# Graph layer, aggregation stage: two sets of scatter matrices, and the second visit of each node tile written ahead of the loop

## The reference

```
xn = layernorm(x)
x  = x + gnn(xn, edges) + mix(xn)
x  = x + moe_ffn(layernorm(x))

gnn(xn): h = xn @ W.T;  e = leaky_relu(h@a_src [src] + h@a_dst [dst])
         alpha = softmax of e over the edges (and one self loop) of each dst
         out[n] = sum over edges with dst = n of alpha * h[src]
         return xn + elu(out + bias)
mix(xn): linear attention, 8 heads, relu(q), relu(k); out / max(q . sum k, 100); projection
moe_ffn: 8 experts, two per row, relu MLP, layernorm, gates
```

## Time and profile before

| | us |
|---|---|
| median of 3 runs | 2688.14 (2682.47 to 2689.73) |
| the profiled execution | 2689.04 |
| its span | 2687.3 |
| PE busy in the span | 2450.9 (91%) |
| DVE busy in the span | 1624.5 (60%) |
| POOL busy in the span | 1283.5 (48%) |

### The profile page before, as it was taken

One profiled execution on the slowest core, in us unless ns is written; L12 is line 12 of the kernel. 1 busy time (PEld: TensorE's weight loads), 2 busy tenths in 40 slices (PEclk: granted clock), 3 DMA queues, 4 the chain that ended last, 5 costly groups with the idle time before them and its releaser, 6 DMA issues. The chain is left out here.

```text
span 2687.3 us, 53608 instructions
## 1 busy us (share of the span) xinstructions
PE 2450.9 (91%) x12032; PEld 1387.6 (52%) x12033; DVE 1624.5 (60%) x4117; ACT 902.2 (34%) x1583; POOL 1283.5 (48%) x1272
## 2 busy tenths in 40 slices
PE   3999899999999889999999999999999639999995
PEld 2555577766666423333444444444444326777773
DVE  2655466664222244466666666666667575889886
ACT  0333344442111100011122222323333426677774
POOL 1444520000000477777776666555545154777774
PEclk9999899999999899999999999999999759999998
DMA  4333733331001477777777776666666355777775
GB/s 177 127 128 123 97 110 101 103 103 33 24 24 32 129 207 213 211 219 227 243 241 224 217 212 207 206 207 197 197 193 205 137 192 102 130 131 132 132 129 82
DMA packets 178069, 409.96 MB, mean 153 GB/s; under 512 B 46749, under 2 KB 46781, under 8 KB 176930
## 3 DMA queue, kind: packets, MB, share of 16 engines
q0 software_dynamic: 90512, 280.63, 40.0%
q1 hardware_dynamic: 59074, 76.65, 10.3%
q10 hardware_dynamic: 28368, 51.41, 5.6%
HBM read 339.65 MB, written 68.82 MB: 152 GB/s over the span
## 5 line engine op out<-in xcount | busy, mean ns | idle before, releaser
L1056 POOL DMA_INDIRECT rows<-h_rows,src_col x784 | 783.8, 1000 | 481.4 <-PE acc_ps L1159 228.8
L1159 PE MATMUL acc_ps<-rows,W 128*128 x1776 | 838.8, 611 | 59.1 <-DVE W L1257 33.2
L1159 PEld LDWEIGHTS acc_ps<-rows,W 128*128 128x128 f32 x1776 | 310.9, 190 | 527.0 <-issue 526.4
L1257 DVE TENSOR_SCALAR W<-window,dst_col,w_col 128x128 f32<-128x128 f32 x888 | 300.3, 372 | 314.5 <-PE acc_ps L1159 263.5
L1635 POOL DMA_INDIRECT out<-y,idx_add x105 | 168.5, 1605 | 112.4 <-issue 47.1
L649 POOL DMA_DIRECT2D alpha_d<-score x1 | 0.6, 573 | 461.8 <-DVE score L967 461.8
L1085 ACT ACTIVATE a_sd<-a_mv,cst 128x1 f32<-128x1 f32 x49 | 14.4, 295 | 606.6 <-DVE a_mv L1323 606.6
L1679 PE MATMUL o_ps<-w,hidT 128*128 x420 | 202.7, 605 | 7.4 <-DVE z L1739 3.2
L1669 PE MATMUL hid_ps<-xsT,w_now 128*128 128x128 f32 x1680 | 206.7, 277 | 0.2 <-issue 0.2
L1669 PEld LDWEIGHTS hid_ps<-xsT,w_now 128*128 128x128 f32 x1680 | 197.8, 194 | 1.0 <-issue 1.0
L773 PEld LDWEIGHTS q_ps<-hxnT,wqkv 128*128 128x128 f32 x1568 | 182.4, 193 | 11.9 <-issue 11.9
(11 more groups left out here) (303 smaller groups left out, 3470.2 us busy)
## 6 DMA issues: line engine op xcount, KB each, us to landing
lo_row<-src_lo SPq DMA_DIRECT2D x98, 256.0 KB, 3.3
xb<-in_x SPq DMA_DIRECT2D x49, 256.0 KB, 2.7
h_rows<-kb SPq DMA_DIRECT2D x49, 256.0 KB
fold_w<-in_x SPq DMA_DIRECT2D x49, 256.0 KB
rows<-h_rows,src_col POOLq DMA_INDIRECT x784, 3.8
a_own<-h_rows ACTq DMA_DIRECT2D x49, 256.0 KB, 3.8
a_xr<-in_x ACTq DMA_DIRECT2D x49, 256.0 KB, 5.2
out<-a_x ACTq DMA_DIRECT2D x49, 256.0 KB, 4.7
```

What stands on the lines that cost most here:

```text
L1056: nc.gpsimd.indirect_dma_start(G[:, n % ROWS, :], None, h_rows, bass.IndirectOffsetOnAxis(ap=src_col[:, n:n + 1], axis=0)).then_inc(row_in ...
L1159: nc.tensor.matmul(acc_ps[s][:], W[:, j, :], G[:, ds(row, 1), :].rearrange("p o d -> p (o d)"), start=(opens and j == 0), stop=(j == VT - ...
L1257: nc.vector.tensor_scalar(W[:, j, :], window[:], dst_col[:, ds(at_tile + j, 1)], w_col[:, ds(at_tile + j, 1)], ALU.is_equal, ALU.mult).the ...
```

## The change

W becomes two sets, `W_open` for the opening visit and `W_rest` for all others. The second visit of each node tile leaves the loop: on PE it stands behind `spread(t+1)` and ahead of `turn` and `denominators`, on DVE behind the opening visit and ahead of `scaled_q`. The loops begin at start + 2. DVE's wait on `row_used` for the two visits in front now asks for the visit two before (`after` = 0), and in the loop for the visit one before (`after` = 1); the semaphore begins 2 * VT ahead in place of VT. The setup stage gives each node tile at least 3 visits, clamps the first edge tile to ET - 3 * VT, and adds 1 + 2 * VT in `used_by`.

```diff
-rout[:, 4:6], rout[:, 0:2], float(ET - 2 * VT), None, ALU.min
+rout[:, 4:6], rout[:, 0:2], float(ET - 3 * VT), None, ALU.min
-rout[:, 3:4], rout[:, 2:3], 2.0, None, ALU.max
+rout[:, 3:4], rout[:, 2:3], 3.0, None, ALU.max
-used_by[:], use_ps[0:1, 0:FREED], float(1 + VT), ...
+used_by[:], use_ps[0:1, 0:FREED], float(1 + 2 * VT), ...
-            W = sb(ag, "W", [P, VT, P])
+            W_open, W_rest = (sb(ag, n, [P, VT, P]) for n in ("W_open", "W_rest"))
 (PE)
                     def visit(v, at_tile, s, opens):
+                        W = W_open if opens else W_rest
...
                                 spread(t + 1, 1 - s)
+                            visit(start + 1, first + VT, s, False)
                             if not isinstance(t, int) or t < NT - 3:
                                 turn(t + 3)
...
-                            with pe.Fori(start + 1, stop) as v:
+                            with pe.Fori(start + 2, stop) as v:
 (DVE)
-                    dve.sem_inc(row_used, VT)
+                    dve.sem_inc(row_used, 2 * VT)
-                    def visit(v, at_tile, opens):
+                    def visit(v, at_tile, W, after):
-                            dve.wait_ge(row_used, VT * v + j + 1)
+                            dve.wait_ge(row_used, VT * (v + after) + j + 1)
-                        if opens:
+                        if W is W_open:
-                            visit(start, first, True)
+                            visit(start, first, W_open, 0)
+                            visit(start + 1, first + VT, W_rest, 0)
                             scaled_q(t, s)
...
-                            with dve.Fori(start + 1, stop) as v:
-                                visit(v, tile_at(v), False)
+                            with dve.Fori(start + 2, stop) as v:
+                                visit(v, tile_at(v), W_rest, 1)
```

More of the change, by code:

```diff
@@ L358, in _ @@
                         step.settle()
-                        step.done(nc.vector.tensor_scalar(rout[:, 4:6], rout[:, 0:2], float(ET - 2 * VT), None, ALU.min))
+                        step.done(nc.vector.tensor_scalar(rout[:, 4:6], rout[:, 0:2], float(ET - 3 * VT), None, ALU.min))
                         step.settle()
@@ L370, in _ @@
                         step.settle()
-                        step.done(nc.vector.tensor_scalar(rout[:, 3:4], rout[:, 2:3], 2.0, None, ALU.max))
+                        step.done(nc.vector.tensor_scalar(rout[:, 3:4], rout[:, 2:3], 3.0, None, ALU.max))
                         assert step.n == 14
@@ L385, in _ @@
                         dve.wait_ge(tri, 2)
-                        nc.vector.scalar_tensor_tensor(used_by[:], use_ps[0:1, 0:FREED], float(1 + VT), C["freed"][0:1, :], ALU.add, ALU.add).then_inc(ints, 1)
+                        nc.vector.scalar_tensor_tensor(used_by[:], use_ps[0:1, 0:FREED], float(1 + 2 * VT), C["freed"][0:1, :], ALU.add, ALU.add).then_inc(ints, 1)
             with ExitStack() as nm:
@@ L542, in load @@
                     for k in range(n):
-                        first = nc.s_assert_within(eng.snap(found[2 * k] & ((1 << AT_BITS) - 1)), 0, ET - 2 * VT,
-                                                   skip_runtime_bounds_check_because="the setup stage takes the minimum with ET - 2 * VT")
+                        first = nc.s_assert_within(eng.snap(found[2 * k] & ((1 << AT_BITS) - 1)), 0, ET - 3 * VT,
+                                                   skip_runtime_bounds_check_because="the setup stage takes the minimum with ET - 3 * VT")
                         stop = eng.snap((visits_to + (found[2 * k] >> AT_BITS)) & 0xFFFF)
```

## The result

The changed kernel took 2706.28 us (median of 6 runs, 2701.97 to 2709.62) where the kernel before took 2688.93 (2682.47 to 2691.84): a ratio of 1.007, 95% interval 1.0058 to 1.0083. Forecast were 2729 us, +40.8; measured are +17.4. The direction, the place and the waiting engine were right; the size was 2.3 times too large. The stated range, 2700 to 2745, does hold the measured time, but not by the main case, whose own range began at 2712: it had been widened for rival B, which didn't happen.

The account below looks back on a forecast made before the run. PE was taken to bound the aggregation from tile 7 on, the gathers before. Spread's waits, 34.9 us in tiles 7 to 39 plus 5.9 in 40 to 48, gave +40.8 on 2689.04, forecast 2729 us allowing for the median; range 2700 to 2745.

Parts of the forecast that it names:

- main case: Aggregation: PE's spread waits for DVE's late qd, +40.8 us, 2729 us, own range 2712 to 2739; chance 0.69.
- rival B: Even openings: their waits absorb the 0.99 us spread wait of each odd tile, +24 us, 2712 us; chance 0.08.
- the tail: Node tiles 40 to 48: later spread, partly given back behind tiles of 3 visits, costs 5.9 us.
- Rival A: Even openings: the wait is for a free W buffer, so W_open removes it, about 2657 us; chance 0.10.
- D: Spread: qd comes in time after all, or the waits hide elsewhere; no change, 2688 +- 8 us; chance 0.07.
- C: PE's clock: added waits halve it in even tiles 8 to 38, 27 us on top, 2756 us; chance 0.06.
- the second visit ahead of scaled_q: DVE: qd ends later, so PE's spread waits 1.13 us in even, 0.99 in odd tiles; 34.9 us over tiles 7 to 39.
- gap in front of W_rest: DVE, between the copy to w_sum and the second visit's first W: taken as 0.53 us, bounds 0.15 and 0.71.

Follow-up runs that it names:

- e2: The changed kernel with the second visit back in the loop on PE and DVE, only the two sets of W kept: 2694.25 us, ratio 1.0009.
- f1: The changed kernel with scaled_q back ahead of the second visit and DVE's x2 block one iteration later: 2658.07 us, ratio 0.9877.
- f2: The kernel before with two sets of W, second visit in the loop, and DVE's x2 block one iteration later: 2674.68 us, ratio 0.9966.
- f3: The kernel before (one set W, second visit in the loop) with DVE's x2 block one iteration later: 2678.68 us, ratio 0.9957.
- e3: The changed kernel with one set W for all visits, the second visit still ahead of scaled_q: 2794.47 us, ratio 1.0387.
- g1: f1 with one set W in place of two: 2799.62 us, ratio 1.0433.
- e4: The changed kernel with PE's spread(t+1) moved behind the second visit, ahead of turn; DVE unchanged: 2686.43 us, ratio 0.9984.
- g2: The changed kernel, order untouched, with DVE's x2 block one iteration later: 2651.4 us, ratio 0.9876.

## Why the prediction was wrong in its size
Of the 23.4 us between forecast and result, 16.7 lie in tiles 7 to 39 and 3.7 in the tail; the rest is of the size by which executions differ in tiles 0 to 6.

**Right.** PE is late at the even openings by DVE's own queue, and W_open alone gives nothing (e2, f1, f2 against f3). No visit was added. `spread` waits for `qd` in some 40 node tiles (39). Three of them are tiles 3, 4 and 6 (0.32, 0.89 and 0.76 us), where the gathers still set the pace; they don't lengthen that stretch, as I had said, and e3's seven waits there barely do. POOL's waits stand nearly as in the earlier trace rows. The wait isn't given back at the even openings (rival B): those waits stand at 1.2 to 1.9 us in tiles 8 to 40, with 0.77 at tile 18 the one exception; from 8 to 40 they sum to 24.2 us against 24.9 before. Rival A is excluded by e2, D by the interval of the result. C did not happen in the changed kernel: one visit at half clock (tile 28, behind a wait of 1.91), as one before (tile 18):
```profile
1769.16 4.54 PE L1160 MATMUL acc_ps<-rows,W_open 128*128 x6 [1.91 <-DVE W_open L1259]
```
```profile
1771.00:1772.00 1.00, 1.00 (x2) 0.39 (x2) 0.85 (x4) 0.99 (x2) 0.27 (x1) 0.50 0.00 0
```
But e3 and g1 show the mechanism at work behind waits of 1.8 to 2.3 us. That agrees with the Trainium skill, TensorE: Matmul & The Clock Gate, Part 1, that idle time takes the array back to half its clock. The length of the wait alone doesn't decide it, so the 1.1 us that I set against the 2.09 was no safe argument: in e4 the visit behind a wait of 2.01 us kept its 2.84 us, and the one behind 1.97 us took 4.53:
```profile
1421.10 2.84 PE L1160 MATMUL acc_ps<-rows,W_open 128*128 x6 [2.01 <-DVE W_open L1259]
...
1515.28 4.53 PE L1160 MATMUL acc_ps<-rows,W_open 128*128 x6 [1.97 <-DVE W_open L1259]
```
What does decide it wasn't tried.

The rule that I weighed for the change, the Trainium skill's Perfetto Trace Analysis, "Identifying Performance Opportunities" (a repeated gap can mean that a buffer is missing), isn't borne out: the gap had 29.4 us with two sets (e2) and 30.7 with one.

**Wrong: the step "the second visit ahead of scaled_q", its price per node tile.** I had 1.13 us in even and 0.99 in odd tiles; measured are 4.14 - 3.40 = 0.74 and 3.94 - 3.54 = 0.40. Piece by piece:

| from the copy's end to `spread` | taken | even | odd |
|---|---|---|---|
| gap in front of W_rest | 0.53 | 0.47 | 0.36 |
| three W | 0.93 | 0.86 | 0.86 |
| gap, w_sum | 0.71 | 0.70 | 0.71 |
| w_sum's end to `qd` | +0.07 | -0.08 | -0.08 |
| `qd` | 0.69 | 0.68 | 0.68 |
| `qd`'s end to `spread` | 0.24 | 0.15 | 0.05 |
| sum | 3.17 | 2.78 | 2.58 |

PE's own arrival is 2.04 us behind the copy's end in even tiles (3.40 - 1.36) and 2.18 in odd ones, and only the rest is cost: 3.17 leaves 1.13 and 0.99, 2.78 and 2.58 leave 0.74 and 0.40. No term is far off, but errors of 0.39 and 0.59 us in the chain count in full against so small a rest. With the measured sizes the same sum gives 16 x 0.74 + 17 x 0.40 = 18.6 us for tiles 7 to 39, and 18.2 were measured; that they agree to less than the 4 us between like runs is luck. (The idle time in front of `spread` reads 0.60 us where it starts 0.74 later, since before the change it began 0.14 us ahead of the recorded end of `total`: 1520.76 against 1520.62 + 0.28.) I named the gap as the largest unknown and gave it bounds of 0.15 to 0.71; the real error was spread over the small terms, all taken a little high, and my main case's own range (2712 to 2739) left them out. One of them stood in my rows: the three W took 0.86 in the earlier trace rows at the opening. That `qd` would start 0.08 us before the recorded end of w_sum stood in none; behind the copy it started 0.07 after. For the last, 0.24 us, I used the distance from the first W to PE's product at the opening; `spread` began 0.05 to 0.15 us behind `qd`, and why it is quicker there the runs don't show.

**The tail**, tiles 40 to 47, was 2.7 us against 6.4 (the forecast 5.9 without the 0.5 that tile 48 was to gain): the same smaller price, and the give-back behind tiles of 3 visits is there. The wait at tile 44 fell from 1.11 to 0.70 and at 47 from 0.69 to 0.23:
```profile
2062.04 2.84 PE L1160 MATMUL acc_ps<-rows,W_open 128*128 x6 [0.70 <-DVE W_open L1259]
...
2108.41 2.84 PE L1160 MATMUL acc_ps<-rows,W_open 128*128 x6 [0.23 <-DVE W_open L1259]
```
I had given tile 47 no such relief; why it fell there wasn't tried.

## What to carry to other kernels
Before adding a buffer, look at what ends the idle time of the engine that should fill it: here it was that engine's own queue. The second set gave nothing by itself, with the long queue (e2) or the shortened one (f2 against f3); what paid was to shorten the queue (f3), and then the second set together with the moved visit (f1 and g2, 1.2% faster). When work is moved ahead of an operation that another engine waits for, the price is the moved length less the time in hand, a difference of two nearly equal numbers: give it a range in which every small term is at its own low and high end, not the one unknown gap alone. And look for the second waiter; the W behind `qd` had less time in hand than `qd` itself.

## What was not expected of the hardware
A wait of 1.8 to 2.3 us once per node tile cost more than its length. e3 had 119.5 us of waits for DVE (87.2 + 32.3), 86 more than the 33.2 of before, and lost 104; g1 had 109.3, 76 more, and lost 116. The rest, 18 and 40 us, went with the granted clock. In the stage it fell to 0.5, mostly for some 3 us, 15 times in e3 and 31 times in g1, nearly always at or just behind such a wait, and once in the kernel before. A fall cost up to 1.7 us (4.50 in place of 2.84), so 14 and 30 more of them are an estimate of up to 24 and 51 us, enough for the rest. Most of e3's 48 waits left the clock as it was. Of its 15 falls 11 are in even node tiles, where an opening wait of 1.2 to 1.6 us stands 5 us ahead: what rival C had named, at a longer second wait. The changed kernel, with 0.3 to 0.9 us at the same place, lost no more than its waits.
